# Four attentions in row and column groups over neighbouring batches, with other products between the rounds of scores of the large cross attention

## The reference, cut to what matters

```python
# stage L0_xattn: 32 heads of 8 features, two softmaxes over 128 keys each
q, k, v = heads(x @ Wq), heads(x @ Wk), heads(x @ Wv); q, k = rope(q), rope(k)
w = softmax(q @ k.T * inv_sqrt_d + attention_mask)
attn_output = w @ v
a_k, a_v = heads(adapter @ Wk), heads(adapter @ Wv)      # adapter is the context
a_scores = tanh(gate) * softmax(q @ a_k.T * inv_sqrt_d)
return (attn_output + a_scores @ a_v) @ Wo
# stages L1_attn and L2_attn: 16 heads of 16 features, causal (L2 with a decay), with biases
# stage L3_attn: 16 heads; the keys of the half of the positions with the highest
#   importance (gelu(x @ W1 + b1) @ W2 + b2) are kept, v is gated by sigmoid(importance)
```

## Time and profile before

| what | value |
|---|---|
| median of 3 runs | 7334.23 us (7329.45 to 7336.71) |
| the profiled execution, its own time | 7358.91 us |
| its span from the first to the last instruction | 7356.8 us |
| PE busy | 4982.6 us, 68% of the span |
| DVE busy | 3711.6 us, 50% |
| ACT busy | 1695.9 us, 23% |
| mean granted clock of PE | 0.767 |

### The profile page before, as it was taken

How to read it: one execution, slowest core, us unless ns; L and a number is a source line. 1 busy time by engine, 2 the same in 40 slices (tenths; PEclk the granted TensorE clock), 3 DMA queues, 4 the chain that set the end, 5 groups by cost and what they waited for, 6 DMA issues and landing times. The chain is left out here.

```text
span 7356.8 us, 76086 instructions
## 1 busy us (share of the span) xinstructions
PE 4982.6 (68%) x27311; PEld 3676.3 (50%) x27312; DVE 3711.6 (50%) x7826; ACT 1695.9 (23%) x3017; POOL 251.2 (3%) x165
## 2 busy tenths in 40 slices
PE   6677777773258677777777773875557677554577
PEld 4455555552146545555555552654446555432366
DVE  4666666667642466656666654224441333234312
ACT  2112222213521132332323321112332111110011
POOL 0000000000001100000000000110000000000000
PEclk8766666665578788988999886886668887556579
DMA  0000000000020000000000000000000000000210
GB/s 19 16 3 3 3 3 3 3 2 20 0 77 0 5 2 1 1 1 1 1 1 1 1 1 10 0 0 14 7 7 12 14 0 0 21 14 0 59 47 11
DMA packets 87403, 70.69 MB, mean 10 GB/s; under 512 B 12384, under 2 KB 82880, under 8 KB 86848
## 3 DMA queue, kind: packets, MB, share of 16 engines
q1 hardware_dynamic: 87360, 70.15, 3.2%
HBM read 68.03 MB, written 2.10 MB: 10 GB/s over the span
## 5 line engine op out<-in xcount | busy, mean ns | idle before, releaser
L646 PE MATMUL bank<-L0x_v,L0x_P 128*128 128x9 f32 x2048 | 383.5, 323 | 136.3 <-DVE L0x_P L570 136.3
L646 PEld LDWEIGHTS bank<-L0x_v,L0x_P 128*128 128x128 f32 x2048 | 372.6, 278 | 146.8 <-DVE L0x_P L570 146.8
L185 PE MATMUL bank<-ident,xn 128*128 128x128 f32 x352 | 93.4, 356 | 392.9 <-DVE xn L177 382.8
L2131 PE MATMUL bank<-L1w_w,L1x_xqT 128*128 128x512 f32 x640 | 316.9, 633 | 28.7 <-DVE L1x_xqT L2307 28.7
L2180 PE MATMUL bank<-L1w_wp,L1x_catT 128*128 128x256 f32 x1024 | 314.6, 462 | 10.8 <-ACT L1x_catT L2241 10.8
L760 PE MATMUL bank<-L0x_mask,ident 128*128 128x512 f32 x512 | 280.8, 696 | 28.6 <-DVE L0x_top L550 12.2
L185 PEld LDWEIGHTS bank<-ident,xn 128*128 128x128 f32 x352 | 46.2, 168 | 487.9 <-DVE xn L177 333.9
L532 ACT ACTIVATE L0x_t<-bank 128x512 f32<-128x512 f32 x256 | 155.3, 607 | 480.7 <-PE bank L646 357.5
L2180 PEld LDWEIGHTS bank<-L1w_wp,L1x_catT 128*128 128x128 f32 x1024 | 237.7, 245 | 52.8 <-ACT L1x_catT L2241 14.6
L567 DVE SCALAR_TENSOR_TENSOR L0x_miss<-L0x_t,L0x_P 128x512 f32<-128x512 f32 x256 | 177.3, 693 | 164.1 <-ACT L0x_P L533 155.9
L550 DVE TENSOR_REDUCE L0x_top<-bank 128x4 f32<-128x512 f32 x256 | 158.8, 682 | 162.8 <-PE bank L631 162.8
(11 more groups left out here) (648 smaller groups left out, 11505.7 us busy)
## 6 DMA issues: line engine op xcount, KB each, us to landing
L3e_wg<-in_L_ffn_Wg SPq DMA_DIRECT2D x8, 704.0 KB, 4.7
L3e_wu<-in_L_ffn_Wu SPq DMA_DIRECT2D x8, 704.0 KB, 6.5
L1w_wp<-in_L_xattn_wproj SPq DMA_DIRECT2D x1, 4096.0 KB, 29.2
L3x_ctxT<-in_ctxT SPq DMA_DIRECT2D x32, 128.0 KB, 2.1
L3e_wd<-in_L_ffn_Wd SPq DMA_DIRECT2D x8, 512.0 KB, 7.8
x_sb<-in_x SPq DMA_DIRECT2D x16, 128.0 KB, 2.2
L0x_ctxT<-in_ctxT SPq DMA_DIRECT2D x16, 128.0 KB, 2.1
L1w_w<-in_L_xattn_wq SPq DMA_DIRECT2D x1, 2048.0 KB, 10.3
```

Source lines behind the costliest of these rows:

```text
L185: last = pe.transpose(out[:, c * 128:(c + 1) * 128], tile[:, c * 128:(c + 1) * 128], kit.ident[:, :])
L646: last = pe.matmul(self.mix_bank[s][:, h * (self.d + 1):(h + 1) * (self.d + 1)], self.P[:, n % self.SLOTS, j * 128:(j + 1) * 128], self.v[ ...
L2131: last = pe.matmul(made_bank[n % 4][:, :], inputs(SOURCE[n], k), w[:, k, 4 * n:4 * n + 4, :], start=(k == 0), stop=(k == C - 1))
```

## The change

`TiledHeads` goes and `QuadRows` comes for L0_xattn; `Heads` stays in the file, and `RowHeads` takes its place in the other three. What is new:

- All four attentions use four groups of 32 rows for scores, for transposed scores and for the `select` product.
- The mask product (`mask_tensor`, not in L3_attn) is cut into pieces of 32 rows by 32 columns, `tile_position=(32 * r, 32 * c)`: 16 small matmuls with 512 moving columns for four banks.
- `mix_tensor` swaps sides: v with 32 columns (16 or 8 features, a one, zeros) is stationary in one of four column groups, P moves with 128 columns. Its result is transposed, so ACT copies it to `raw` and PE turns it over (`turn_raw_tensor`).
- The correction by tanh is gone: one exponential a block.
- q, kM and v exist twice; a turn of the loop does the shifts of b, the scores of b+1 and the entry (norm, turn, products) of b+2. In `RowHeads` a turn also finishes b-1. POOL spreads no keys; ACT spreads those of the context.
- The mask of L0_xattn comes from DRAM in four copies of its rows, one DMA of 128 partitions x 4 KB a batch.

```diff
-class TiledHeads(Heads):
...
+def staged(eng, turn):
+    for b in range(-2, 0):
+        turn(b, b % 2, b)
+    with eng.Fori(0, (B - 2) // 2) as t:
+        for i in range(2):
+            turn(t * 2 + i, i, i)
+    for b in range(B - 2, B):
+        turn(b, b % 2, b)
...
+class QuadRows:
+    ROWS, SLOTS, WIDE, ROUNDS, H, d = 4, 4, 32, 4, 32, 8
...
+    def mask_tensor(self, pe, mask):
+        pe.sem_inc(self.masking, 1)
+        for c in range(4):
+            for r in range(self.ROWS):
+                rows = self.rows_of(r)
+                pe.matmul(self.work_bank[r][32 * c:32 * c + 32, :], self.kit.ident[rows, rows],
+                          mask[rows, c, :].unsqueeze(1).to_broadcast([32, 4, 128]), start=True, stop=False,
+                          tile_position=(32 * r, 32 * c))
+    def scores_tensor(self, pe, b, odd, i, mask):
+        s, c = divmod(i, C)
+        if i >= 1:
+            wait(pe, self.top_found, b, 4 * i)
+        if s == 0:
+            self.mask_tensor(pe, mask)
+        for r in range(self.ROWS):
+            rows = self.rows_of(r)
+            pe.matmul(self.work_bank[r][:, :], self.qT[odd][rows, c, :], self.kM[odd][s][rows, c, :, :],
+                      start=(s == 1), stop=True).then_inc(self.scored.sem, 1)
+    def shifts_tensor(self, pe, b, odd, i, mask_T):
+        s, c = divmod(i, C)
+        if i >= 1:
+            wait(pe, self.p_ready, b, 4 * i)
+        else:
+            wait(pe, self.top_found, b)
...
+    def mix_tensor(self, pe, b, odd, i):
+        s, c = divmod(i, C)
+        if i >= 1:
+            wait(pe, self.raw_ready, b, i)
+        for r in range(self.ROWS):
+            wait(pe, self.p_ready, b, 4 * i + r + 1)
+            for j in range(self.SLOTS):
+                last = pe.matmul(self.raw_bank[32 * j:32 * j + 32, r * 128:(r + 1) * 128], self.v[odd][s][:, 16 * c + 4 * r + j, :],
+                                 self.P[:, i % 2, r, j * 128:(j + 1) * 128], start=True, stop=True, tile_position=(0, 32 * j))
+        last.then_inc(self.mixed.sem, 1)
...
+    def attend_tensor(self, pe, b, odd, mask_T, enter):
+        for i in range(self.ROUNDS):
+            self.shifts_tensor(pe, b, odd, i, mask_T)
+            if i == 0:
+                enter()
+            if i >= 1:
+                self.mix_tensor(pe, b, odd, i - 1)
+            if i >= 2:
+                self.turn_raw_tensor(pe, b, i - 2)
+        self.mix_tensor(pe, b, odd, self.ROUNDS - 1)
+        self.turn_raw_tensor(pe, b, self.ROUNDS - 2)
...
+                for i in range(at.ROUNDS):
+                    if ahead:
+                        at.scores_tensor(pe, b + 1, 1 - odd, i, mask[:, 1 - odd, 0, :, :])
+                    if i == 0 and entering:
+                        wait(pe, normed, b + 2)
+                        turn_tensor(kit, pe, bank[0], kit.xn).then_inc(turned.sem, 1)
+                    if i == 0 and here:
+                        at.turn_raw_tensor(pe, b, at.ROUNDS - 1)
...
+                    if i == 1 and entering:
+                        wait(pe, xT_ready, b + 2)
+                        project(kit, pe, bank[1][:, 0:D], kit.xnT, wv)
+                        project(kit, pe, bank[1][:, D:2 * D], ctxT, wv).then_inc(v_made.sem, 1)
...
+                    if i == 2 and ahead:
+                        if here:
+                            wait(pe, y_read, b)
+                        at.turn_top_tensor(pe, b + 1, 0)
...
+class RowHeads:
...
+    def leave_tensor(self, pe, b, wo, y_made):
+        wait(pe, self.o_ready, b)
+        turn_tensor(self.kit, pe, self.out_bank, self.o).then_inc(self.o_turned.sem, 1)
+        wait(pe, self.oT_ready, b)
+        project(self.kit, pe, self.y_out, self.oT, wo).then_inc(y_made.sem, 1)
...
```

More of the change, by code:

```diff
@@ L796, in _ @@
+            staged(pe, turn)
         @block.scalar
@@ new lines, in turn @@
+            def turn(b, odd, at_b):
+                here, ahead, entering = 0 <= at_b < B, 0 <= at_b + 1 < B, at_b + 2 < B
+                step.restart()
+                if ahead:
+                    heads_of(b + 1, 1 - odd)
+                if entering:
+                    norm_vector(kit, dve, b + 2, kit.xn[:, :]).then_inc(normed.sem, 1)
+                if here:
+                    for i in range(at.ROUNDS - 1):
+                        at.normalize_vector(dve, b, i, gate, step)
+                for i in range(at.ROUNDS):
+                    if ahead:
+                        at.maxima_vector(dve, b + 1, i)
+                    if i == 0 and here:
+                        at.normalize_vector(dve, b, at.ROUNDS - 1, gate, step)
+                    if i == 1 and ahead:
+                        at.split_vector(dve, b + 1, 0, step)
+                    if i == 2 and here:
+                        wait(dve, y_made, b)
+                        add_residual(kit, dve, b, at.y_out).then_inc(y_read.sem, 1)
+                if ahead:
+                    at.split_vector(dve, b + 1, 1, step)
@@ L877, in masked_attention, with pipelined @@
+def pipelined(eng, turn):
+    for b in range(-2, 1):
+        turn(b, b % 2, b)
+    with eng.Fori(0, (B - 4) // 2) as t:
+        for i in (1, 2):
+            turn(t * 2 + i, i % 2, i)
+    for b in range(B - 3, B + 1):
+        turn(b, b % 2, b)
 def masked_attention(kit, name, prefix, swap, load_ahead=None):
@@ L949, in _, with turn @@
-            turn(0)
-            front(0)
-            with pe.Fori(0, B - 1) as b:
-                batch(b)
-            batch(B - 1, last=True)
+                return lambda pe: at.mask_tensor(pe, maskb[:, i, :, :])
+            def turn(b, odd, at_b):
+                here, behind, ahead, entering = 0 <= at_b < B, 1 <= at_b <= B, 0 <= at_b + 1 < B, at_b + 2 < B
+                if here:
+                    at.shifts_tensor(pe, b, odd, add_mask(1))
+                if behind:
+                    at.leave_tensor(pe, b - 1, wo, y_made)
+                if here:
+                    if ahead:
+                        wait(pe, at.v_ready, b + 1)
+                    at.mix_tensor(pe, b, odd)
+                if ahead:
+                    at.scores_tensor(pe, b + 1, 1 - odd, add_mask(0))
+                if entering:
+                    wait(pe, normed, b + 2)
+                    turn_tensor(kit, pe, at.turn_bank, kit.xn).then_inc(turned.sem, 1)
+                if here:
+                    wait(pe, at.raw_ready, b)
+                    if behind:
+                        wait(pe, y_read, b - 1)
+                    at.turn_raw_tensor(pe, b)
+                if entering:
+                    wait(pe, xT_ready, b + 2)
+                    project_T(pe, at.qk_bank, wq, kit.xnT)
+                    project_T(pe, at.qk_bank[:, D:2 * D], wk, kit.xnT).then_inc(qk_made.sem, 1)
+                    if ahead and not here:
+                        wait(pe, at.v_ready, b + 1)
+                    project(kit, pe, at.v_out, kit.xnT, wv).then_inc(v_made.sem, 1)
+                if ahead:
+                    at.turn_top_tensor(pe, b + 1)
@@ L955, in _ @@
+            pipelined(pe, turn)
         @block.scalar
@@ L1015, in _ @@
[L1015 to L1021 removed]
+                    for i in range(2):
+                        last = dve.tensor_scalar(at.kM[odd][:, c, i, :], at.qk_bank[:, D + c * 128:D + (c + 1) * 128],
+                                                 bcol[:, 1, c:c + 1], at.headmask[:, i:i + 1], ALU.add, ALU.mult)
@@ L1024 @@
+            pipelined(dve, turn)
 class L1xWeights:
```

824 lines of the change are left out of this document (526 added, 298 removed).

## The result

| what | before | after |
|---|---|---|
| median | 7335.47 us (4 runs, 7329.45 to 7373.29) | 5706.25 us (4 runs, 5683.92 to 5711.86) |
| the profiled execution, its span | 7358.9, 7356.8 | 5711.9, 5710.1 |
| PE, DVE, ACT busy | 68%, 50%, 23% | 67%, 52%, 28% |

The ratio is 0.7765, with a 95% interval of 0.7732 to 0.7798. On the profiled basis the change took off 1647 us where the sum said 1467: 180 more.

The account below looks back on a forecast made before the run. Waits and a low clock, not one engine, were taken to bound the kernel. Savings of 803 + 399 + 265 = 1467 us off 7358.9 gave 5892, as a median 5870; range 5700 to 6300.

Parts of the forecast that it names:

- the sum: Over the attention stages: 803 in L0_xattn, 399 in L1_attn and L2_attn, 265 in L3_attn, together 1467 us saved.
- the likeliest case: Whole kernel: the forecast by itself, 5700 to 6050 us, chance 0.60.
- Column groups do not overlap: Rival for masks and mixes in all four attentions: column groups run in series, 432 us more, 6300; chance 0.17.
- Each matmul drains: Rival: each column-grouped matmul drains before the next starts, 2865 us more, 8735, slower than before; chance 0.02.
- The clock stays low: Rival: PE's clock stays at 1.2 GHz in the attention stages, 531 us more, 6400; chance 0.17.
- The prices of the blocks at full clock: PE blocks in L0_xattn at clock 1.00: mask 1.14 us, `select` 0.5, mix of 16 heads 1.17.
- the y_read wait: Score half of L0_xattn, round 2: PE waits for the residual on DVE and the turn of first maxima, 0.8 us.
- all at 1.00: Whole kernel with every turn at full clock: 5734 us; a time better than 5700 had chance 0.04.
- The ends of the stages: Taken off the savings: 10 us in L0_xattn, 8 each in L1_attn and L2_attn, 10 in L3_attn.
- about 0.2 of its time is at the low level. I take 0.2: Low-clock share of a turn, from L1_xattn: raises L0_xattn from 37.8 to 41.4 us, L1_attn and L2_attn to 13.0.
- the ring's sum at full clock: Block times added per turn at clock 1.00: L0_xattn 37.8 us, L1_attn and L2_attn 11.3, L3_attn 15.5.
- 64 passes of 0.69 are gone: L0_xattn: DVE loses its tanh-correction passes, 44 us a turn, leaving some 22 us of DVE work, covered.

Follow-up runs that it names:

- e3: The changed kernel with masks as whole-array products, four per score round, in place of 16 pieces each: 5886.5 us.
- e4: The changed kernel with the 16 heads of a mix in L0_xattn ordered column group by column group instead of turning through the four groups: 5757.1 us.
- e8: The changed kernel with L0_xattn's wait for the residual and turn of the first maxima moved behind the fourth score round: 5674.0 us.
- e7: The changed kernel with L0_xattn's turns of xn and raw and its context and v products ahead of the first score round: 5781.2 us.
- e10: The changed kernel with L0_xattn's loop of seven iterations of two turns written out on PE, ACT and DVE: 5686.7 us.
- e1: The kernel before the change, without the correction of the exponential by tanh: 7137.0 us, L0_xattn stage 1261.6 us.
- e9: The changed kernel with the correction by tanh put back into L0_xattn: 6319.3 us, L0_xattn stage 1259.2 us.
- e5: The changed kernel with one useless DVE pass a turn in L0_xattn, ahead of the residual PE waits for: 5713.5 us.
- e2: The kernel before with only L0_xattn changed; L1_attn, L2_attn and L3_attn are the old ones: 6525.1 us.
- e6: The changed kernel with three useless DVE passes a turn in L0_xattn, ahead of the last maxima of rounds 0, 1 and 3: 5721.9 us.
- e12: The changed kernel with L0_xattn's turn of the first maxima behind the fourth score round and its loop written out: 5668.0 us.

## What the prediction had right, and the step that failed

The direction, the mechanism and the rivals came out as the likeliest case had them. *Column groups do not overlap* is refuted by the blocks of 1.15 and 1.08, and e3 and e4 show what it would have cost. *Each matmul drains* falls with it. *The clock stays low*: 0.97 to 1.00. The prices of the blocks at full clock held, and the y_read wait was foreseen (0.8; e8 gives 0.6 to the hold). The low end of the range was "all at 1.00", 5734, and a little; the time came out below that. Turn by turn (16, 32 and 16 turns), as forecast less as measured:

- L0_xattn 41.4 - 37.45, L1_attn and L2_attn 13.0 - 10.65, L3_attn 16.8 - 14.1: 63 + 75 + 43 = 181 us.
- The ends of the stages, beyond 16 turns: L0_xattn 39.9 us where it was 14.0, so 26 more and not 10; L1_attn and L2_attn 25.5 and 26.7 where they were 33.2 and 34.6, 8 less each and not 8 more; L3_attn 14 more and not 10. Together 12 us in favour of the change; the rest of the program took 14 back.

So the mechanism was right as far as it was tested, and a term of the sum was mis-sized. No run takes away the overlap of neighbouring batches or the row groups alone, and of the 811 us of L1_attn to L3_attn only the share of the masks was measured (e3: 16.9 and 13.6). How the rest divides between overlap, row groups and the new mix is argued and not shown.

**The step that failed: "about 0.2 of its time is at the low level. I take 0.2",** read from the mean clock of L1_xattn, another stage. It was worth 16 x 3.6 + 32 x 1.7 + 16 x 1.3 = 133 us. In the new loops the clock is 1.00 in L1_attn and L2_attn and 0.99 in L3_attn, so nearly all of their 75 us is gone; in L0_xattn it is 0.97, falls in 8 of 14 turns, and e8 puts its price at 0.6 a turn, 10 us for 58. Two things were wrong in it. The share came from a neighbour with a similar busy share, when my own rows had the better guide, the hole ahead of the low clock (2.55 us in the earlier trace rows; the new turn had none above 1.9). That guide too is rough, as holes of 1.90 were followed by a low clock in about half of the turns, but only for a block or two. And the price of a low clock was that of a whole turn: the blocks that run low lie under DVE's maxima. e7 had a share of the low level of about 0.24 (clock 0.88), near what I had assumed, and it cost 2.3 us a turn and not 4.4.

**The second: the ring's sum at full clock was too long,** by about 58 us: in part because blocks were added with their whole lengths, where the next block starts 0.06 to 0.18 us before the profile's end of the last, in the rows above. A round of shifts without a mask takes 3.53 (520.27 to 523.80) and not 3.8, one with a mask 4.6 to 4.7 and not 4.9. In L1_attn the ring reads 10.65 and not 11.3; in L3_attn a turn is 14.1 where the ring was 15.5, and which of its terms was too long was not looked into. In L0_xattn two things hide most of it, the loop's jump, which I did not have (e10: 8.6 us), and what the clock still costs; the turn without either is 36.23 (549.73 to 585.96) where I had 37.8.

I had no price of the correction alone, and none was needed for the sum; but "64 passes of 0.69 are gone" reads as if it were the saving itself. By e1 and e9 it is worth 228 us in the old order and 1259.2 - 639.1 = 620 in the new one.

## What to carry to other kernels

Two changes that each relieve one of two engines in turn can be worth far more together than the sum (230 + 228 against 850), so a trial of one alone says little. A low granted clock is no share to be spread over all work: look for the hole ahead of it, ask whether the new order still has a hole like it, and charge only the low blocks that nothing covers. For a ring, add start-to-start distances, not lengths; and look at every second turn, as a loop over two turns can hide both its own jump and a clock that falls in some turns only.

## What the runs showed of the hardware

- 16 pieces of 32 by 32 in f32, 512 columns each, take 1.15 us for all 32 records where four whole-array products of the same output take 3.67, in either order of the pieces. Four matmuls in a row into one column group take 2.46 for 1.08.
- The clock fell behind a hole of 2.68 us in 12 of 14 turns (e5), behind one of 1.90 in 8 (changed kernel), 6 (e2, the same stage) and 9 of 14 (e6, with longer holes elsewhere), behind one of 1.82 in 11 of 14 (e10), and behind one of 1.50 in none of 14 (e8, e12). So a hole's length alone does not decide. Nor does it at the loop's jump in e8: of the holes of 1.79 to 2.10 us there, one of 1.96 was followed by low blocks, and the mask behind one of 1.88 runs at full speed.
- The jump back of a loop cost 36.94 - 35.62 = 1.32 us in L0_xattn (e8; without it, in e12, all turns but one are 35.68), and at most 0.3 in L1_attn, whose turns alternate between 10.79 and 10.51.
